# A four-stage network on one core: in its attention stage, the turning of the next rows behind the second scores, values ahead of moments, the gate one place later

## The reference

```
x = x + attention(layernorm(x), adj)     # 8 heads of 32, the stage of this change
x = x + lstm(layernorm(x))
x = x + graph_layers(layernorm(x), adj)
x = x + fp8_matmul(layernorm(x))

def attention(inputs, adj, ...):
    q, k, v = inputs @ Wq + bq, inputs @ Wk + bk, inputs @ Wv + bv   # split into 8 heads
    logits = q k^T / sqrt(32), where(adj > 0, logits, -1e9)
    attn   = softmax(logits)
    return relu((attn v) @ Wo + bo)
```

## Time and profile before

| | us |
|---|---|
| median of 3 runs | 2901.27 (2898.44 to 2902.7) |
| the profiled execution | 2900.7 |
| its span | 2898.9 |
| PE busy over the span | 2620.3 (90%) |
| DVE busy | 2051.5 (71%) |
| ACT busy | 1924.1 (66%) |
| POOL busy | 1622.4 (56%) |

### The profile page before, as it was taken

The page is one execution under the profiler, slowest core; times in us unless marked ns, Lnnn a source line. Parts: engine busy times, 40 slices in busy tenths (PEclk is TensorE's granted clock), DMA queues, the critical chain, the costliest instruction groups (busy, mean ns, idle before and its releaser), DMA issues. The chain is left out here.

```text
span 2898.9 us, 117977 instructions
## 1 busy us (share of the span) xinstructions
PE 2620.3 (90%) x44129; PEld 2385.9 (82%) x44224; DVE 2051.5 (71%) x6871; ACT 1924.1 (66%) x5044; POOL 1622.4 (56%) x2677
## 2 busy tenths in 40 slices
PE   6999999978888888869999999999999999999956
PEld 5676676767777777759999999999999999999955
DVE  6888888854444444437777777877777788888868
ACT  4666666654444444437888888778777778888734
POOL 5777777720000000016888886666666677777755
PEclk9999999999999999988999999999999999999989
DMA  3111111000000000021000001100000110000003
GB/s 90 37 36 36 36 36 36 29 8 13 13 13 13 13 13 13 13 53 48 24 25 27 24 25 44 47 7 9 9 9 9 30 30 9 9 9 9 8 8 109
DMA packets 110839, 74.60 MB, mean 26 GB/s; under 512 B 51505, under 2 KB 109361, under 8 KB 110513
## 3 DMA queue, kind: packets, MB, share of 16 engines
q1 hardware_dynamic: 96800, 61.03, 7.4%
q10 hardware_dynamic: 13968, 12.72, 1.5%
HBM read 51.68 MB, written 22.02 MB: 25 GB/s over the span
## 5 line engine op out<-in xcount | busy, mean ns | idle before, releaser
L1631 PE MATMUL g_H<-g_hT_upper,g_w_upper 128*128 128x256 f32 x1536 | 461.2, 300 | 0.2
L1631 PE MATMUL g_H<-g_hT_upper,g_w_rest 128*128 128x256 f32 x1536 | 434.8, 283 | 0.0
L1631 PE MATMUL g_H<-g_hT_rest,g_w_upper 128*128 128x256 f32 x1536 | 434.6, 283 | 0.0
L1659 PE MATMUL g_F<-g_w_upper,g_act_upper 128*128 128x256 f32 x1408 | 410.3, 291 | 8.0 <-DVE g_act_rest L1399 4.7
L1184 ACT ACTIVATE g_act_raw<-g_H,g_small 128x256 f32<-128x256 f32 x768 | 319.6, 471 | 124.5 <-PE g_H L1631 123.4
L756 POOL COPY l_xt<-seq 128x64 f32 x256 | 60.8, 238 | 598.8 <-PE l_O L767 595.0
L1659 PE MATMUL g_F<-g_w_upper,g_act_rest 128*128 128x256 f32 x1408 | 395.7, 281 | 0.0
L1659 PE MATMUL g_F<-g_w_rest,g_act_upper 128*128 128x256 f32 x1408 | 395.4, 281 | 0.0
L330 ACT ACTIVATE a_probs<-a_S,a_nmax 128x256 f32<-128x256 f32 x512 | 236.8, 480 | 131.3 <-DVE a_nmax L428 104.1
L1399 DVE TENSOR_TENSOR g_act_rest<-g_act_raw,g_act_upper 128x512 fp32r<-128x512 f32 x352 | 267.8, 762 | 46.0 <-ACT g_act_upper L1189 40.5
L795 ACT ACTIVATE l_ic<-l_G 128x128 f32<-128x128 f32 x256 | 71.1, 278 | 341.8 <-PE l_G L767 341.8
(11 more groups left out here) (223 smaller groups left out, 8135.0 us busy)
## 6 DMA issues: line engine op xcount, KB each, us to landing
gmask<-masks ACTq DMA_DIRECT2D x97, 128.0 KB, 2.0
x<-in_x_dram SPq DMA_DIRECT2D x32, 256.0 KB, 3.1
a_adj<-in_adj_dram SPq DMA_DIRECT2D x32, 256.0 KB, 2.8
hidden<-l_hs SPq DMA_DIRECT2D x512, 16.0 KB, 1.4
seq<-hidden SPq DMA_DIRECT2D x32, 256.0 KB, 2.7
out_dram<-q_res SPq DMA_DIRECT2D x32, 256.0 KB, 2.1
masks<-gmask SPq DMA_DIRECT2D x32, 128.0 KB, 1.7
g_w_raw<-in_L_gnn_W_dram SPq DMA_DIRECT2D x6, 512.0 KB, 3.8
```

The source lines that it names most:

```text
L1631: last = pe.matmul(hidden_bank[m // 2][:, m % 2 * N:(m % 2 + 1) * N], w[:, c, m * P:(m + 1) * P], x[:, c, :], start=(c == 0 and k == 0), s ...
L1659: last = pe.matmul(ff_bank[:, it * D:(it + 1) * D], x[:, m, it * P:(it + 1) * P], w[:, m, :], start=(m == 0 and it == 0 and k == 0), stop= ...
```

## The change

On each engine the same functions are called, in another order; no instruction is added or removed but some of the sequencer's own register steps.

```
 ACT graph                      late_out(b, 2)
-                               xnT_out(b + 1)
                                xn2T_out(b - 2)
                                late_out(b, 3)
+                               xnT_out(b + 1)

 DVE graph                      early_out(b, 0)
+                               early_out(b, 1)
+                               heads_out(b - 1)
+                               v_out(b)
                                moments1(b + 2)
-                               heads_out(b - 1)
-                               early_out(b, 1)
-                               v_out(b)
+                               largest(b, 4), largest(b, 5)
                                xnT_rest_out(b + 1)
-                               largest(b, 4) to largest(b, 7)
-                               gate(b - 1)
+                               largest(b, 6), largest(b, 7)
                                early_out(b, 4)
                                q_out(b + 1)
-                               residual(b - 1)
+                               gate(b - 1)
                                early_out(b, 5)
+                               residual(b - 1)
                                k_out(b + 1)

 PE graph                       turn_xn2(b - 2)
-                               turn_xn(b + 1)
                                turn_probs(b, 3)
                                scores(b, 1)
+                               turn_xn(b + 1)
                                project(b - 1)
```

More of the change, by code:

```diff
@@ L359, in graph @@
                     late_out(b, 2)
-                    if exists(b + 1):
-                        xnT_out(b + 1)
                     if exists(b - 2):
@@ L364, in graph @@
                     late_out(b, 3)
+                    if exists(b + 1):
+                        xnT_out(b + 1)
                     for h in range(HG, H):
@@ L488, in graph @@
                     early_out(b, 0)
+                    early_out(b, 1)
+                    if exists(b - 1):
+                        heads_out(b - 1)
+                    v_out(b)
                     if exists(b + 2):
                         moments1(b + 2)
-                    if exists(b - 1):
-                        heads_out(b - 1)
-                    early_out(b, 1)
-                    v_out(b)
+                    for h in range(HG, HG + 2):
+                        largest(b, h, i)
                     if exists(b + 1):
                         xnT_rest_out(b + 1)
-                    for h in range(HG, H):
+                    for h in range(HG + 2, H):
                         largest(b, h, i)
-                    if exists(b - 1):
-                        gate(b - 1)
                     early_out(b, 4)
@@ L504, in graph @@
                     if exists(b - 1):
+                        gate(b - 1)
+                    early_out(b, 5)
+                    if exists(b - 1):
                         residual(b - 1)
-                    early_out(b, 5)
                     if exists(b + 1):
@@ L664, in graph @@
                         turn_xn2(b - 2)
+                    turn_probs(b, 3)
+                    scores(b, 1)
                     if exists(b + 1):
                         turn_xn(b + 1)
-                    turn_probs(b, 3)
-                    scores(b, 1)
                     if exists(b - 1):
```

## The result

| | before | changed |
|---|---|---|
| median of runs, us | 2900.82 (4 runs, 2898.44 to 2902.7) | 2858.91 (4 runs, 2855.47 to 2860.01) |
| profiled span, us | 2898.9 | 2853.7 |

The ratio is 0.9854, with a 95% interval of 0.9837 to 0.9871; a second measurement later gave 2858.58 against 2901.8, 0.9854 again (0.9841 to 0.9866). The forecast was 2865.3 with a gain of 36.0; 41.9 and 43.2 were gained. The time lies in the range (2858 to 2879), at its fast end and only 0.9 us inside it.

A forecast was written before the change was run, and what follows sets the result against it. The attention loop was taken as bound by DVE's work plus its holes. A gain of 1.16 us over 31 batches, 36.0, took the profiled 2900.7 to 2864.7, with 0.6 for the median 2865.3; range 2858 to 2879.

The forecast's parts named there:

- Period of the loop as DVE's work plus its holes: Attention loop, 18.09 us: DVE's work plus three holes; stretches head 0 to head 4 (9.00) and head 4 to keys (6.98).
- Head 0 to head 4, gain 1.16: DVE's first stretch: next rows turned behind the second scores bring head 4 at 308.21 instead of 309.37.
- the 0.50 of a turning: PE: one turning taken as 305.86 - 305.36 = 0.50, putting head 3 one turning later, at 306.36.
- The witness of batch 31: Batch 31, without next rows, already goes the changed PE order: head 0 to head 4 takes 7.64; forecast kept 7.84.
- Head 4 to the keys, 6.97: DVE's second stretch: L397 moves in, the 0.57 hole before the keys goes; keys at 315.2 instead of 316.35.
- The margins: Slack before head 4 to the keys loses time: L397 0.5, queries 0.05, keys 0.04.
- Batches 0, 1 and 30: Batches outside the 28 of the loop that also turn next rows; each taken to gain 1.16 as an estimate.
- the forecast's own sign: Attention stage: forecast is wrong if it gets shorter by less than 27 us or more than 42.
- Rival 1: PE passes from scores to turning in 1.37, not 1.08: gain 0.87 a batch, 27 us, 2874; chance 0.25 with its like.
- Rivals 2: Second scores on PE don't come earlier, head 4 stays at 309.37: no change, 2900; chance 0.05.
- rival 3: L397 blocks DVE because turned rows come late: 0.3 a batch slower, 9 us, 2911; chance 0.05.
- The rule on two SBUF inputs: DVE's residual beside POOL's normalising: by the skill's exclusion rule DVE is held 0.06, making the sum 31 x 1.10 = 34.

The follow-up runs named there:

- before, heads early: Kernel before with DVE taking the heads ahead of the moments, nothing else; 2899.76 us against 2901.13, ratio 0.9995.
- Moments first: Changed kernel with DVE's moments back behind the first copy, ahead of heads, copy 1 and values; 2864.15 us against 2899.24 before, ratio 0.9884.
- L397 first: Changed kernel with DVE's L397 ahead of the maxima of head 4 again; 2908.46 us against 2901.13 before, ratio 1.0027.
- gate back: Changed kernel with DVE's gate ahead of copy 4 again and residual ahead of copy 5; 2876.08 us against 2899.24 before, ratio 0.9922.
- Only DVE's order: Changed kernel with PE and ACT put back in the order before; 2879.65 us against 2899.24 before, ratio 0.9932.
- only PE's and ACT's order: Kernel before with PE's and ACT's new order, DVE in the order before; 2916.71 us against 2899.24, ratio 1.006.
- residual early: Changed kernel with DVE's gate and residual ahead of the queries' copy; 2899.18 us (one run) against 2901.8 before.
- copy 5 on ACT: Changed kernel with copy 5 moved to ACT and DVE's reciprocals ahead of the keys' copy; 2855.24 us against 2901.8 before, ratio 0.9837.

## Why the prediction was right, point by point

- Period of the loop as DVE's work plus its holes, with the two stretches: right. It is what every experiment answered to, including the two that were slower than before.
- Head 0 to head 4, gain 1.16: the mechanism was right, the size was 1.29 (7.71). The term that was off is the 0.50 of a turning, which stands in the sum twice: in the start of the turning of b-2 (305.86) and in "head 3 one turning later". It was read from a distance in which PE was slightly held by the heads; the turning takes 0.43 to 0.44 ("before, heads early"). That is 0.13 a batch, 4 of the missing 6 us. "Moments first" shows the same from the other side: there the heads and copy 1 come late again, the two distances are 0.50 and 0.51, and head 4 comes at 7.90. The witness of batch 31 (7.64), kept in the forecast only as a bound, was the better number.
- The new waits, about 0.3 before L418 and 1.0 before head 4: 0.23 and 0.77. L397 doesn't wait: right.
- Head 4 to the keys, 6.97: right, 6.96. The margins were as narrow as said. For the queries it is 0.10 (4.18 against the way of 4.08 in "L397 first"). The keys are set by PE and not by DVE's row: they start 0.68 behind the residual (293.70 - 293.02), which needs only 0.60, and 2.78 behind the queries. So a move that puts the queries 0.6 later, as in "gate back", loses the whole 0.6.
- Batches 0, 1 and 30 "the same, as an estimate", 31 none: 3.5 forecast, 6.5 found. The keys' copies of batches 1 and 2 come 41.56 - 39.25 = 2.3 and in all 59.37 - 55.25 = 4.1 us earlier, batch 30 gives 0.7, and from the last keys' copy to the LSTM it takes 1.7 less. This 1.7 is hardly the change's: 1.5 of it is TensorE's clock, which fell in the tail of the one profile and not of the other, as is shown below the windows. PE's windows of the kernel before, behind the first scores and in the tail:

```profile
33.00:36.00 3.00, 0.85 (x13) 0.45 (x6) 2.68 (x14) 1.53 (x8) 2.84 (x4) 1.00 0.58 145
36.00:39.00 3.00, 3.00 (x19) 3.00 (x18) 1.99 (x7) 1.33 (x6) 0.33 (x1) 0.63 0.52 167
...
606.00:609.00 3.00, 2.00 (x20) 1.07 (x24) 1.21 (x6) 2.36 (x5) 1.43 (x3) 0.63 0.00 0
```

  and of the changed kernel in the same places:

```profile
33.00:36.00 3.00, 1.73 (x15) 1.73 (x16) 3.00 (x16) 2.84 (x12) 2.69 (x6) 1.00 0.34 88
36.00:39.00 3.00, 2.81 (x24) 2.46 (x23) 2.06 (x5) 1.81 (x7) 2.84 (x4) 1.00 0.15 45
...
564.00:567.00 3.00, 2.31 (x37) 1.15 (x35) 1.41 (x6) 2.52 (x5) 1.16 (x2) 1.00 0.00 0
```

  Before, the clock fell to 1.2 GHz for a part of the window (a mean of 0.63 of full speed), in the first place after PE had been busy for 0.85 of 3 us; the weighing of the last batch took 3.15 us there against 1.93 in the changed kernel. But the fall is not bound to the order of work. In the second profile of the changed kernel the clock fell too, to a mean of 0.59 in 24 to 27 us and of 0.50 in 564 to 567 us; the weighing of the last batch took 3.53 and the tail 34.40 us, where it was 32.90 in the first profile of the same kernel and 34.64 before. "Only DVE's order", "only PE's and ACT's order" and "moments first", which had no fall there, took 32.74 to 33.23. In the first batches, by contrast, the gain stands with and without a fall: from the keys of batch 0 to those of batch 2 it takes 33.94 and 33.37 us in the two profiles of the changed kernel, 38.10 before. Why these two batches give 4.1 where 2.3 was forecast stays open.
- Size of the whole: by the forecast's own sign (an attention stage shorter by more than 42 us is wrong) it falls just outside, since the LSTM's first step comes 43.6 earlier in both profiles (625.6 against 582.0); without the 1.7 of the tail it would be 41.9. (In the second profile the tail gave only 0.2, but its first keys already stood 1.2 earlier than in the first.) The measured time is inside the range, by 0.9 us. The mechanism was right and the sum too low; that the time still lies in the range is in part luck.
- The rest of the first profile's 45.2 us: from the LSTM's last step to the end it took 1612.3 us, against 1614.6 before and 1614.9 in the second profile of the changed kernel. So this is the chance of one execution (it was also the fastest of its four) and not the change; the LSTM itself took 0.4 to 0.7 us more.
- Rival 1 (turning behind scores as late as the project was, 1.37): PE needed 1.08 (285.41 to 286.49), as taken. Rivals 2 and 3 didn't occur, but rival 3's place is live: L397's wait for ACT is what made "only PE's and ACT's order" and "L397 first" slower than before.
- The rule on two SBUF inputs, weighed there as 0.06 a batch: the residual started 0.60 behind its predecessor while POOL still ran for 0.32, and lasted 0.69. It wasn't held. Its successor, the keys' copy, waits for PE anyway.

## What to carry to other kernels

Where several engines run their lists in order, write the period as one way over the engines plus one closed row of work on the fullest, and price each move by what it takes from these; the parts of a reordering aren't additive, and half of one can be slower than none. Before using a distance of two starts as a duration, look for a second place where it is shorter: a distance with no wait listed can still hold one. When the last hole of a row closes, check the next way beside it to a tenth of a microsecond, since that is what a further move will run into.

## What the runs showed of the hardware

Two engines with SBUF operands beside each other. POOL's normalising (two instructions of 1.22 us, L217) and DVE's residual (two SBUF inputs, 0.68 alone) overlap in several of the kernels. In "gate back" the residual starts 0.29 after POOL's second instruction and lasts 0.80, its successor starts 0.72 later instead of 0.60, and POOL's pair keeps its 2.43. In "residual early" it starts in POOL's first instruction, as DVE's and POOL's rows show:

```profile
291.66 0.68 DVE L455 TENSOR_TENSOR a_xn<-a_O,a_bo_row 128x512 f32<-128x512 f32 x1
292.48 0.69 DVE L460 SCALAR_TENSOR_TENSOR x<-a_xn,x 128x512 f32 x1
293.09 0.99 DVE L404 TENSOR_SCALAR a_qT<-a_Q,a_qscale,a_bqs 128x256 f32<-128x256 f32 x2
```

```profile
291.64 2.63 POOL L217 TENSOR_SCALAR a_xn<-x,a_mv,a_rstd 128x256 f32<-128x256 f32 x2
```

There DVE is undisturbed (0.69, and it didn't wait for POOL's first instruction, which had some 0.4 to go) and POOL's pair takes 2.63 instead of 2.43. In batch 1 of "gate back" the residual starts 1.09 behind POOL's first instruction, just ahead of the second, and the pair takes 2.87:

```profile
53.86 0.68 DVE L460 SCALAR_TENSOR_TENSOR x<-a_xn,x 128x512 f32<-128x512 f32 x1
```

```profile
52.77 2.87 POOL L217 TENSOR_SCALAR a_xn<-x,a_mv,a_rstd 128x256 f32<-128x256 f32 x2
```

So the two directions differ. When the residual comes into a running POOL instruction, DVE loses 0.13 at most. When POOL's second instruction is due while the residual runs, POOL loses more the later the residual started: 0.20 with a start 0.84 behind the first instruction, 0.44 with 1.09, and 0.51 with 1.21 (batch 1 of "copy 5 on ACT"). Each is what POOL would lose if it went on 0.52 to 0.58 behind the residual's start (1.09 + 0.57 - 1.22 = 0.44), close to the 0.60 after which DVE's next instruction starts. The Trainium skill, "SBUF — State Buffer", section "Who interferes with whom", says that the later of two such instructions waits for the whole of the first; that would have held the residual 0.93 in "gate back". The measurement decides here: with DVE as the later one there was no such wait; with POOL as the later one the trace agrees. POOL's rows are rough, so the hundredths stay open.

An instruction that reads what the one directly ahead of it on DVE wrote, with a semaphore between, starts later than the 0.60 that these instructions take from DVE with another instruction between them. From gate to residual it is 0.82 in the loop of "residual early", 0.82 and 0.92 in the two iterations of a pair of "copy 5 on ACT" (307.13 to 307.95 is the shorter one), and 0.71 to 0.73 in the batches of both that are written out. In the loop an instruction set between the two costs therefore 0.38 (2 x 0.60 - 0.82), not 0.60. What makes the loop's distance longer than that of the written-out batches, and 0.92 of 0.82, wasn't followed; the sequencer's register steps, which only the loop has, are a likely cause that isn't shown.
